# Perceiver layer kernel: the first layer's maximum pass taken by pairs of key tiles

## What is computed

```
q = (x @ Wq).reshape(B, Nq, H, D)
k = (context @ Wk).reshape(B, Nkv, H, D)
v = (context @ Wv).reshape(B, Nkv, H, D)
sim = jnp.einsum('bihd,bjhd->bhij', q, k) * SCALE
attn = jax.nn.softmax(sim, axis=-1)
out = jnp.einsum('bhij,bjhd->bihd', attn, v).reshape(B, Nq, H * D)
```

## Time and profile before

| | us |
|---|---|
| median of 3 runs | 1390.9 |
| lowest, highest | 1390.6, 1392.61 |
| span of the profiled execution, first to last instruction | 1386.1 |
| first pass of layer one: TensorE's first matmul of it, start | 22.95 |
| same pass: start of the first turning of the maxima | 131.70 |

### The profile page before, as it was taken

The page is one execution under the profiler, slowest core; times in us unless marked ns, Lnnn a source line. Parts: engine busy times, 40 slices in busy tenths (PEclk is TensorE's granted clock), DMA queues, the critical chain, the costliest instruction groups (busy, mean ns, idle before and its releaser), DMA issues.

```text
span 1386.1 us, 30350 instructions
## 1 busy us (share of the span) xinstructions
PE 1329.7 (96%) x10061; PEld 974.1 (70%) x10061; DVE 789.5 (57%) x1384; ACT 653.3 (47%) x1181; POOL 279.2 (20%) x412
## 2 busy tenths in 40 slices
PE   6998999999999999999778999999899999999988
PEld 5666666666666666666556888888777777777775
DVE  5999343343433433335627888888856556555442
ACT  1554333333333333332204777777566666666520
POOL 1664100000000000000024777777200000000110
PEclk8999999999999999999899999999999999999999
DMA  3443600000010010102262444444344532222162
GB/s 125 122 124 95 247 23 30 23 25 28 23 30 23 24 29 23 30 15 84 106 278 69 159 159 159 159 157 157 113 151 157 180 101 83 91 76 90 60 241 91
DMA packets 58826, 137.19 MB, mean 99 GB/s; under 512 B 6608, under 2 KB 7024, under 8 KB 56240
## 3 DMA queue, kind: packets, MB, share of 16 engines
q1 hardware_dynamic: 50160, 92.83, 20.9%
q0 software_dynamic: 8640, 44.00, 8.5%
HBM read 110.97 MB, written 25.82 MB: 99 GB/s over the span
## 4 chain that ended last, share of the span: by engine, by line
PE 82%; DVE 7%; issue 5%; DMA 4%; POOL 1%; ACT 1%; DVEq 0%; SPq 0%; POOLq 0%; ACTq 0%
PE ps L569 64%; PE ps L753 7%; PE ps L749 7%; DMA raw<-ctx_in 3%; PE ps L557 1%; DMA ring<-ex_in 1%; POOL t_ha L334 1%; DVE wide L1217 1%; PE ps L1065 1%; DVE wide L1222 0%; PE ps L898 0%; PE ps L692 0%; PE ps L920 0%; PE ps L1041 0%; DVE probs L1353 0%
## 5 line engine op out<-in xcount | busy, mean ns | idle before, releaser
L454 ACT ACTIVATE probs<-ps 128x512 f32<-128x512 f32 x588 | 319.4, 601 | 241.9 <-PE ps L569 241.9
L1299 DVE TENSOR_TENSOR wide<-wide,probs 128x1024 f32<-128x1024 f32 x97 | 118.9, 1225 | 304.1 <-ACT probs L454 304.1
L438 ACT CAST wide<-ps 128x512 bf16<-128x512 f32 x294 | 163.6, 595 | 84.2 <-PE ps L569 84.1
L1217 DVE TENSOR_TENSOR wide<-ps,wide 128x512 f32<-128x512 f32 (+1 forms) x196 | 185.9, 948 | 25.5 <-PE ps L569 25.2
L569 PE MATMUL ps<-q_ha,t_ha 128*128 128x512 f32 x392 | 171.6, 438 | 7.4 <-DVE q_le L1141 3.8
L1222 DVE TENSOR_TENSOR wide<-wide 128x512 bf16<-128x512 bf16 (+1 forms) x196 | 143.5, 732 | 16.1 <-ACT wide L438 8.1
L446 ACT COPY v_sb<-ps 128x512 f32<-128x512 f32 x98 | 57.6, 588 | 198.1 <-PE ps L569 198.1
L569 PEld LDWEIGHTS ps<-q_ha,t_ha 128*128 128x128 f32 x392 | 75.3, 192 | 58.7 <-issue 25.3
L749 PEld LDWEIGHTS ps<-probs,v_sb 128*64 128x64 f32 x1568 | 83.6, 136 | 35.3 <-ACT probs L454 34.9
L749 PE MATMUL ps<-probs,v_sb 128*64 128x128 f32 x1568 | 107.0, 279 | 0.0
L753 PE MATMUL ps<-probs,v_sb 128*32 128x128 f32 x3136 | 105.7, 276 | 0.0
(11 more groups left out here) (388 smaller groups left out, 2524.5 us busy)
## 6 DMA issues: line engine op xcount, KB each, us to landing
raw<-ctx_in SPq DMA_DIRECT2D x147, 256.0 KB, 2.6
v_mem<-probs SPq DMA_DIRECT2D x49, 256.0 KB, 2.1
k_mem<-probs SPq DMA_DIRECT2D x49, 256.0 KB, 2.3
wide<-k_mem SPq DMA_DIRECT2D x49, 256.0 KB, 2.9
wide<-v_mem SPq DMA_DIRECT2D x49, 256.0 KB, 2.6
ring<-ex_in POOLq DMA_DIRECT2D x8, 1152.0 KB, 11.0
ring<-ex_in POOLq DMA_DIRECT2D x13, 512.0 KB, 4.8
wa<-ex_in POOLq DMA_DIRECT2D x4, 1152.0 KB, 9.8
```

What stands on the lines that cost most here:

```text
L438: act.copy(half16[:, c:c + 512], ps[:, back_bank(layer, q) + u, :]).then_inc(sem(f"half{layer}"), 1)
L454: act.activation(probs[:, j * 2048 + u * 512:j * 2048 + (u + 1) * 512], ps[:, s_bank[layer][u], :], ACT.Exp).then_inc(sem(f"exp{layer}"), 1)
L1217: dve.tensor_tensor(r, ps[:, b:b + half // 512, :].rearrange("p b n -> p (b n)"), r, ALU.max)\
L1299: dve.tensor_tensor(run[:, 0:1024], run[:, 0:1024], e, ALU.add).then_inc(sem("lsum"), 1)
```

## The change

In layer one the unit of the pass becomes the group. TensorE writes a group's four scores to four banks that lie together (0 to 3 for slot 0, 4 to 7 for slot 1). VectorE takes the first of the four (tile 0, heads 0 to 3) from PSUM as before. ScalarE (`keep_three`, new) copies the second bank by one instruction of 512 columns and the third and fourth by one of 1024, when the fourth is written. VectorE takes the maximum of all three copies by one bf16 instruction of 1536 columns into `three`, which lies in `run[:, 1024:1792]`. `half16` has a buffer of 1536 columns for each slot. After the last group two maxima of 512 columns bring the four accumulators to the two that are turned; these take the place of the widening copy. The clearing memset of the bf16 accumulator is 1536 columns wide, before 512. TensorE waits for a group's first bank on `front0`, for the second and for the third with the fourth on `half0`. Layer two's instructions are the same as before.

```diff
+            def keep_three(g, slot, first):
+
+                if not first:
+                    act.wait_ge(sem("run0"), g - 1)
+                c = slot * 1536
+                act.wait_ge(sem("s1b_0"), 2 * g + 1)
+                act.copy(half16[:, c:c + 512], ps[:, 4 * slot + 1, :]).then_inc(sem("half0"), 1)
+                act.wait_ge(sem("s1b_0"), 2 * g + 2)
+                act.copy(half16[:, c + 512:c + 1536], ps[:, 4 * slot + 2:4 * slot + 4, :].rearrange("p b n -> p (b n)"))\
+                   .then_inc(sem("half0"), 1)
...
-                            if n >= units:
+                            if layer == 0:
+                                o = ps[:, 4 * slot + 2 * j + n, :]
+                                if not first and j == 0 and n == 0:
+                                    pe.wait_ge(sem("front0"), g - 1)
+                                elif not first and n == 1 - j:
+                                    pe.wait_ge(sem("half0"), 2 * g - 3 + j)
+                            elif n >= units:
...
+            three = run[:, 1024:1792].bitcast(BF16)
...
-                    link(dve.memset((run[:, 0:half], half16[:, 2048:2048 + half])[w], LOWEST))
+                    link(dve.memset((run[:, 0:half], half16[:, 2048:2048 + half] if layer == 1 else three)[w], LOWEST))
...
+                def maxima0(g, slot, first):
+                    dve.wait_ge(sem("s1a_0"), g + 1)
+                    if not (first and slot == 0):
+                        dve.wait_ge(sem("front0"), g)
+                    dve.tensor_tensor(run[:, 0:512], ps[:, 4 * slot, :], run[:, 0:512], ALU.max).then_inc(sem("front0"), 1)
+                    dve.wait_ge(sem("half0"), 2 * g + 2)
+                    if not (first and slot == 0):
+                        dve.wait_ge(sem("run0"), g)
+                    dve.tensor_tensor(three, half16[:, slot * 1536:(slot + 1) * 1536], three, ALU.max)\
+                       .then_inc(sem("run0"), 1)
...
+                if layer == 0:
+                    groups(dve, maxima0)
+                    dve.wait_ge(sem("front0"), GROUPS)
+                    dve.wait_ge(sem("run0"), GROUPS)
+                    dve.tensor_tensor(run[:, 0:512], run[:, 0:512], three[:, 512:1024], ALU.max)\
+                       .then_inc(sem("lanes_half"), 1)
+                    dve.wait_ge(sem("lanes_half"), 1)
+                    dve.tensor_tensor(run[:, 512:1024], three[:, 0:512], three[:, 1024:1536], ALU.max)\
+                       .then_inc(sem("lanes"), 1)
```

More of the change, by code:

```diff
@@ L475, in body @@
                         keep_keys(g + 1, 1 - slot, first and slot == 0)
-                    for j in range(GT):
+                    if layer == 0:
+                        keep_three(g, slot, first)
+                    for j in range(GT if layer == 1 else 0):
                         q = tile_buffer(layer, slot, j)
-                        keep_half(layer, g * GT + j, q, first and (slot == 0 or layer == 0))
+                        keep_half(layer, g * GT + j, q, first and slot == 0)
                         if layer == 1 and j == 0 and not last:
@@ L673, in scores1 @@
                                 last.then_inc(sem(f"s1b_{layer}"), 1)
-                            elif n == units - 1:
+                            elif n == units - 1 and (layer == 1 or j == 0):
                                 last.then_inc(sem(f"s1a_{layer}"), 1)
@@ L694, in turn_lanes @@
                     return last
-                pe.wait_ge(sem(f"front{layer}"), TILES)
+                if layer == 0:
+                    pe.wait_ge(sem("lanes_half"), 1)
+                else:
+                    pe.wait_ge(sem("front1"), TILES)
                 turn_lanes(range(heads // 2), (2, 6)[layer]).then_inc(sem("lanes_f"), 1)
@@ L1205, in cross @@
                     queries1()
-                run16 = half16[:, 2048:2048 + half]
+                run16 = half16[:, 2048:2048 + half] if layer == 1 else three
+                def maxima0(g, slot, first):
[8 more added lines that the diff above has]
+                       .then_inc(sem("run0"), 1)
                 def maxima(g, slot, first):
@@ L1223, in maxima @@
                            .then_inc(sem(f"run{layer}"), 1)
-                groups(dve, maxima)
-                dve.wait_ge(sem(f"run{layer}"), TILES)
-                dve.tensor_copy(run[:, half:2 * half], run16).then_inc(sem("lanes"), 1)
+                if layer == 0:
+                    groups(dve, maxima0)
[6 more added lines that the diff above has]
+                       .then_inc(sem("lanes"), 1)
+                else:
+                    groups(dve, maxima)
+                    dve.wait_ge(sem("run1"), TILES)
+                    dve.tensor_copy(run[:, half:2 * half], run16).then_inc(sem("lanes"), 1)
                 if layer == 0:
```

## The result

The changed kernel takes **1402.47 us** (median of 4 runs, 1401.42 to 1406.04) against 1390.81 for the kernel before (median of 4 runs beside it, 1390.6 to 1392.61): the ratio is 1.009, 95% interval 1.0073 to 1.0106, that is 10 to 15 us slower. The forecast was 1399.9, slower, with a range from 1386 to 1404. The profiled execution's span goes from 1386.1 to 1399.5, +13.4.

The account below looks back on a forecast made before the run. Layer one's first pass was taken as bound by the load and GpSimd loop, 2.15 us a group, not VectorE. Rounds +10.0, short gaps -2.3, start +0.3, end +1.0: +9.0 on 1390.9 gives 1399.9 us, range 1386 to 1404.

Parts of the forecast that it names:

- The direction: Layer one's first pass: slower, because the wide maximum is requested before `t_ha` and lengthens GpSimd's loop; chance 0.66.
- Rival 1: The wide maximum's request falls behind the start of `t_ha`, so GpSimd loses nothing: 1386.4 us, chance 0.18.
- The rounds: A slot's turns through load and GpSimd rounding, groups 8 to 48: 20 x 0.50 = +10.0 us, before 2.3 given back.
- the short gaps: About 10 of 40 groups where the request falls into `t_ha` and GpSimd is not held: -2.3 us.
- the gap itself: Time from the end of `t_ha` to the slot's next `t_e` on GpSimd, kept at 2.88 us in the mean.
- The hold: How long the wide maximum runs on behind the end of `t_e`, keeping `t_ha` waiting: taken as 0.85 us.
- the prediction's own test: The maximum gets in ahead of `t_ha` if the time from `t_ha` to next `t_e` exceeds 3.38 - 0.57 = 2.81 us.
- The start: First groups of the pass, up to group 8, where TensorE sets the pace: +0.3 us.
- the end: Behind the last `t_ha`, until TensorE turns the maxima: 4.96 us in place of 3.93, so +1.0.
- The turning near 141.5: Expected sign at the pass's end: TensorE turns the maxima near 141.5 us on the timeline instead of 131.70.
- The prediction's estimate by the page: By the skill's whole-instruction rule each hit costs the loop the wide maximum's full 0.97 us: 4.1 us more, 1404.
- That is also the most that the change can win: Best possible outcome: 1386.4 us, or 1385.9 even if VectorE set the pace, since TensorE needs 2.0 us a group.

Follow-up runs that it names:

- the first trace: Profiled execution of the changed kernel as it is, in the main measurement: 1402.47 us, ratio 1.009 to the kernel before.
- the second: Trace of the changed kernel run once more, unchanged, beside the follow-up kernels: 1399.24 us, ratio 1.0078 to the kernel before.
- the kernel with the pairs and four buffers: The changed kernel with four load buffers in layer one's first pass in place of two: 1379.42 us, ratio 0.9924 to the kernel before.

## Why the prediction came out as it did

**What bounds the kernel**: right. The pass was set by the loop of load and GpSimd, though VectorE was busy for 100% and TensorE's weight loads waited for it. The kernels with less VectorE work (1389), with more GpSimd work (1404) and with four buffers (1378) show it from three sides.

**The direction**, and with it the choice among rivals: right, and by the mechanism that was named: the maximum is asked for inside `t_e` and gets in ahead of `t_ha`. Rival 1, the request behind the gap, was put 0.07 us away. In the first trace the request lies 0.1 to 0.5 behind `t_e`, 0.31 in the mean, so 0.26 from the border at 0.57; in the second it is 0.43 in the mean, 0.14 from it, and five groups crossed it. That the margin came out wider than 0.07 was not foreseen: the request was sooner and the gap longer than taken, and both errors happened to fall on the safe side.

**The terms**: the total was +9.0; at the turning of the maxima the trace has +14.3, the span +13.4, the median +11.7. The rounds were to give 10.0 - 2.3 = 7.7 and gave 12.7; two terms, the short gaps and the gap itself, make up nearly all of the difference.

- The hold was taken as 0.85 (end of the maximum behind the end of `t_e`); it is 0.86. `t_ha` in the row is 1.37.
- The short gaps were to give back 2.3 us, with 10 of 40 counted. **This term was mis-sized.** In the first trace it is nothing, because no gap was short: the shortest is 2.85, and the prediction's own test was 2.81. In the second 8 gaps are under 2.81, and 4 of them let `t_ha` go free (the fifth escape followed on two others). The other 4 did not, because the request comes sooner than the 3.38 that was taken: 3.35 behind the end of the slot's last `t_ha` in even groups and 3.26 in odd ones (`t_ha` of group 19 ends at 69.80 and the maximum is asked for at 73.06). TensorE starts 0.13 and 0.05 behind that `t_ha`, not 0.14; the copy of 1024 was priced right, 1.01.
- The gap was kept at 2.88. It was 3.00 in the first trace, 2.91 in the second: 20 x 0.12 = 2.4 us in the one, 0.6 in the other. The loads themselves were slower in the first, 2.7 us from issue to landing in the median between 32 and 120 us, against 2.6 in the second. The fear that it would shrink was unfounded; that it depends on how loads are spaced was tried and fell.
- The start gave +0.5 (taken +0.3), the end +1.2 (taken +1.0): the two instructions that join the four accumulators cost what the rows said, 0.69 each.
- Of the signs that were named, a held wide maximum was to take 1.0 to 1.1; it takes 0.96 to 1.37, 1.15 in the mean, because it asks earlier inside `t_e`. The turning near 141.5 did not follow from the sum, which gives 140.7; it came at 146.01.

**The rule of the Trainium skill** (SBUF — State Buffer, "SBUF: two separate sides") is that the two engines take the shared ports in turn, for a whole instruction, whoever is first. The trace of the kernel with the earlier copy agrees on the order in 39 of its 41 groups, down to leads of 0.02 us; in the other two, told there, it was not the one that asked first. On the price the measurement decides: the wide maximum takes 0.96 alone, and costs `t_ha` 0.77. The prediction's estimate by the page, 1404, is nearer to 1402.47 than its own 1399.9, but not for its reason: the time beyond 1399.9 came from the longer gap and the missing short gaps, and the hold of 0.86 was nearly the 0.85 that was taken.

**"That is also the most that the change can win"**, 1386, was not passed by any kernel with two buffers: the best median is 1388.52. But the figure behind it, TensorE's 2.0 us a group, was too high: unstarved it needs 1.87.

## What to carry to other kernels

An engine at 100% in every slice can still be slack, if it is held up on others' behalf: ask which wait closes a loop, and test it by giving the busy engine less to do. One wide instruction in place of several narrow ones saves on its own engine, but it may hold another engine for its whole width; where that other engine stands in a loop, the price is per meeting and not per share of time. Open the loop first (here two buffers that lay free, 1390.6 to 1377.9) and see what is then left to gain.

## What was not expected of the hardware

- A bf16 maximum of two SBUF operands and a GpSimd instruction do not share: the one that starts 0.03 us or more ahead goes first and the other waits it out, but for the cases of the next point. What was new is the price: a 0.60 us rounding that was held took 0.84, 0.97 and 1.37 behind a maximum of 512, 768 and 1536 columns, which take 0.41, 0.56 and 0.96 alone, so it loses 0.17 to 0.19 less than the maximum's own time. A maximum that reads PSUM, 0.68 us, neither held nor was held.
- When GpSimd goes from one instruction to the next without a pause, a maximum that waits for the first does not always get in between: between `t_e` and `t_ha` it always did, but in 8 cases of other pairs (6 in the kernel with more GpSimd work, 2 in that with the earlier copy) it waited out both. Why is open.
- Such meetings lock in phase, but not firmly: in the first trace all 42 groups from number 7 on had one, in the second 5 of 41 escaped, and in the kernel with the pairs and four buffers no `t_ha` was held from number 1 on.
- VectorE's busy time holds the time in which it is kept out: the same 512-column maximum shows 0.41 or up to 0.90.
